# First layer of a graph propagation: blocks' places looked up half a round ahead, in PSUM banks of their own

## The reference

```python
def _propagate(all_emb, rows, cols, vals):
    acc = all_emb
    x = all_emb
    for _ in range(N_LAYERS):          # 3
        x = jax.ops.segment_sum(vals[:, None] * x[cols], rows, num_segments=N_NODES)
        acc = acc + x
    return acc / (N_LAYERS + 1)
...
rating = users_emb @ items_emb.T
rating = rating + bias_user[users] + bias_item.T
return jax.nn.sigmoid(rating)
```

## Time and profile before

| | us |
|---|---|
| median of 3 runs | 7561.97 |
| lowest and highest | 7558.92, 7563.39 |
| profiled execution | 7557.79 |
| its span | 7556.0 |

### The profile page before, as it was taken

The page is one execution under the profiler, slowest core; times in us unless marked ns, Lnnn a source line. Parts: engine busy times, 40 slices in busy tenths (PEclk is TensorE's granted clock), DMA queues, the critical chain, the costliest instruction groups (busy, mean ns, idle before and its releaser), DMA issues.

```text
span 7556.0 us, 213021 instructions
## 1 busy us (share of the span) xinstructions
PE 4726.8 (63%) x73184; PEld 4198.0 (56%) x73188; DVE 5009.9 (66%) x11593; ACT 4137.8 (55%) x10708; POOL 2330.0 (31%) x2100
## 2 busy tenths in 40 slices
PE   5201111057777777887566666788666666678879
PEld 4200110046666666887556666688655666668854
DVE  9999999964444445999544444599844444469970
ACT  0155445333333335999444444699744444479976
POOL 0144434034444443000454455200055555520000
PEclk9755555555556655555676666655577776665559
DMA  9300000034444444554344444455444444445536
GB/s 345 148 0 0 0 0 0 0 94 135 133 137 134 135 134 129 142 145 120 127 138 132 136 137 137 133 145 146 110 137 138 135 138 135 134 132 145 145 105 241
DMA packets 750538, 918.14 MB, mean 122 GB/s; under 512 B 71784, under 2 KB 607881, under 8 KB 750363
## 3 DMA queue, kind: packets, MB, share of 16 engines
q1 hardware_dynamic: 658540, 665.77, 31.9%
q0 software_dynamic: 91520, 250.84, 8.9%
q10 hardware_dynamic: 434, 1.05, 0.1%
HBM read 529.36 MB, written 388.09 MB: 121 GB/s over the span
## 4 chain that ended last, share of the span: by engine, by line
PE 34%; issue 23%; DVE 17%; DMA 11%; ACT 10%; another core or an unknown queue 2%; POOL 2%; DVEq 1%; ACTq 0%; SPq 0%; POOLq 0%
PE psum L1420 28%; DMA ring<-posts 11%; ACT ring L630 5%; ACT ring L628 3%; DVE store L987 3%; DVE store L985 2%; DVE total L817 2%; DVE store L995 2%; DVE store L996 2%; POOL ring L711 2%; PE psum L1415 2%; DVE ring L1174 1%; ACT ring L627 1%; PE psum L1471 1%
## 5 line engine op out<-in xcount | busy, mean ns | idle before, releaser
L1420 PE MATMUL psum<-ring 128*128 128x64 bf16 x45504 | 2524.4, 228 | 1187.7 <-issue 1077.5
L1420 PEld LDWEIGHTS psum<-ring 128*128 128x128 bf16 x45504 | 2256.0, 121 | 1437.2 <-issue 1411.9
L618 ACT ACTIVATE ring<-psum,ring 128x64 f32<-128x64 f32 x7584 | 1654.6, 340 | 2207.2 <-DVE ring L1197 889.8
L740 POOL DMA_INDIRECT posts<-ring x1896 | 1866.9, 985 | 1968.6 <-ACT ring L618 1531.6
L1170 DVE COPY ring<-store 128x384 bf16 x1896 | 522.2, 275 | 1472.6 <-PE psum L1420 714.5
L1174 DVE TENSOR_SCALAR ring<-ring,lane_f 128x512 bf16<-128x512 bf16 x3792 | 1177.7, 352 | 0.0
L1445 PE MATMUL psum<-ring 128*128 128x64 bf16 x15168 | 1002.6, 244 | 0.0
L1445 PEld LDWEIGHTS psum<-ring 128*128 128x128 bf16 x15168 | 965.1, 167 | 0.0
L630 ACT ACTIVATE ring<-ring 128x1024 bf16<-128x1024 uint8 x948 | 943.5, 1042 | 0.0
L1439 PE MATMUL psum<-ring 128*128 128x64 bf16 x7584 | 616.9, 249 | 238.4 <-ACT psum L634 224.8
L1439 PEld LDWEIGHTS psum<-ring 128*128 128x128 bf16 x7584 | 555.8, 158 | 302.5 <-issue 300.4
(11 more groups left out here) (239 smaller groups left out, 4207.9 us busy)
## 6 DMA issues: line engine op xcount, KB each, us to landing
ring<-posts SPq DMA_DIRECT2D x474, 516.0 KB, 3.9
ring<-lanes_d SPq DMA_DIRECT2D x474, 512.0 KB
out<-ring SPq DMA_DIRECT2D x200, 250.0 KB, 2.0
posts<-store SPq DMA_DIRECT2D x2, 20640.0 KB, 115.8
posts<-store SPq DMA_DIRECT2D x2, 20124.0 KB, 88.6
posts<-ring POOLq DMA_INDIRECT x1896
ring<-runs_d SPq DMA_DIRECT2D x158, 128.0 KB
user_rows<-total SPq DMA_DIRECT2D x1, 1568.0 KB, 5.9
```

The costliest lines, as they stand in the source:

```text
L618: last = nc.scalar.activation(of, psum[:, n, b * F:(b + 1) * F], ACT.Copy, scale=vring[:, h, c * BLOCK + b:c * BLOCK + b + 1])
L740: pool.indirect_dma_start(out=posts[:, :], out_offset=bass.IndirectOffsetOnAxis(ap=dring[:, h, c:c + 1], axis=0), in_=msg[:, n, :], in_off ...
L1420: last = pe.matmul(psum[:, n, b * F:(b + 1) * F], hot[c][:, k, b * P:(b + 1) * P], xt[c][:, (k * PARTS + x) * F:(k * PARTS + x + 1) * F], ...
```

## The change

In the first layer the look-up of a half's places moves ahead by half a round. VectorE makes the one-hot runs of the next half after the third one-hot block of this half; TensorE does the next half's look-up straight after this half's fourth sum, into bank 4 or 5 (by half), which no sum uses; VectorE reads the shifts after the half's own four one-hot blocks, without waiting for a sum, and writes the places to `dest_m`, from where they are copied to `dring` as in the other layers. So that banks 4 and 5 are free, the first layer's sums go to banks 0 to 3 in turn: TensorE waits for the message of four blocks back, not eight. The first look-up stands ahead of the loop, and the last round is written out behind it, since it has no next one. Layers 1 and 2 keep eight banks.

```diff
@@ ScalarE, messages
-                            last = nc.scalar.activation(of, psum[:, n, b * F:(b + 1) * F], ACT.Copy,
+                            last = nc.scalar.activation(of, psum[:, n if layer else c, b * F:(b + 1) * F], ACT.Copy,
@@ VectorE
+                def run_hots(h, landed, looked):
+
+                    dve.wait_ge(s_drow[h], landed)
+                    if looked is not None:
+                        dve.wait_ge(s_looked, looked)
+                    for k in range(2):
+                        last = nc.vector.tensor_scalar(rhot[h][:, k, :], runs_r[h], lane_f[:, k:k + 1], None, ALU.is_equal)
+                    last.then_inc(s_rhot, 1)
+
+                def place(i, h):
+
+                    dve.wait_ge(s_looked, i * 2 + (h + 1))
+                    nc.vector.tensor_reduce(found[:, h, :], psum[:, 4 + h, 0:4 * PARTS].rearrange("p (c x) -> p c x", x=PARTS),
+                                            AX.X, ALU.add).then_inc(s_found, 1)
+                    dve.wait_ge(s_found, i * 2 + (h + 3))
+                    nc.vector.tensor_tensor(dest_m[:, bass.ds(i * 8 + h * 4, 4)], found[:, h, :], order_m[:, bass.ds(i * 8 + h * 4, 4)],
+                                            ALU.add).then_inc(s_placing, 1)
+
-                            if layer == 0 and c == 0:
-                                dve.wait_ge(s_drow[h], i * 16 + 16)
-                                for k in range(2):
-                                    last = nc.vector.tensor_scalar(rhot[h][:, k, :], runs_r[h], lane_f[:, k:k + 1], None, ALU.is_equal)
-                                last.then_inc(s_rhot, 1)
+                            if layer == 0 and c == 2 and not (final and h == 1):
+                                run_hots(1 - h, i * 16 + 16 * (h + 1), None if first and h == 0 else i * 2 + h)
+                        if layer == 0:
+                            place(i, h)
                         dve.wait_ge(s_msg, i * 8 + (done + h * 4 + 4))
+                        if layer == 0:
+                            dve.wait_ge(s_placing, i * 2 + (h + 1))
                         if not first:
                             dve.wait_ge(s_scat[h], i * 64 + layer * BODIES * 64)
                         if layer == 0:
-                            dve.wait_ge(s_sent, i * 8 + (h * 4 + 5))
-                            nc.vector.tensor_reduce(found[:, h, :], psum[:, h * 4, 256:256 + 4 * PARTS].rearrange("p (c x) -> p c x", x=PARTS),
-                                                    AX.X, ALU.add).then_inc(s_found, 1)
-                            dve.wait_ge(s_found, i * 2 + (h + 3))
-                            nc.vector.tensor_tensor(dring[:, h, :], found[:, h, :], order_m[:, bass.ds(i * 8 + h * 4, 4)], ALU.add).then_inc(s_placing, 1)
-                            dve.wait_ge(s_placing, i * 2 + (h + 1))
-                            nc.vector.tensor_copy(dest_m[:, bass.ds(i * 8 + h * 4, 4)], dring[:, h, :])
-                        else:
-                            nc.vector.tensor_copy(dring[:, h, :], dest_m[:, bass.ds(i * 8 + h * 4, 4)])
+                            dve.sem_inc(s_dvepace, 1)
+                        nc.vector.tensor_copy(dring[:, h, :], dest_m[:, bass.ds(i * 8 + h * 4, 4)])
...
                 if layer == 0:
+                    run_hots(0, 16, None)
                     send(0, True)
-                with dve.Fori(0 if layer else 1, BODIES) as i:
-                    send(i, False)
+                    with dve.Fori(1, BODIES - 1) as i:
+                        send(i, False)
+                    send(BODIES - 1, False, True)
+                else:
+                    with dve.Fori(0, BODIES) as i:
+                        send(i, False)
@@ TensorE
-                with pe.Fori(0, BODIES) as i:
+                def look_up(i, h):
+
+                    _, at_d = nc.values_load_multi_w_load_instructions(
+                        super_d[0:1, bass.ds(i * 8 + h * 4, 4)], engines=(mybir.EngineType.PE,), min_val=0,
+                        max_val=(SUPERS - 1) * 2 * PARTS, skip_runtime_bounds_check_because="the chip clamps each above")
+                    pe.wait_ge(s_rhot, i * 2 + (h + 3))
+                    pe.wait_ge(s_found, i * 2 + (h + 1))
+                    for m in range(4):
+                        for k in range(2):
+                            last = pe.matmul(psum[:, 4 + h, m * PARTS:(m + 1) * PARTS], rhot[h][:, k, m * P:(m + 1) * P],
+                                             dflat[:, bass.ds(at_d[m] + k * PARTS, PARTS)], start=(k == 0), stop=(k == 1))
+                    last.then_inc(s_looked, 1)
+
+                def sums(i, final):
+
                     for n in range(8):
                         c = n % 4
-                        if layer == 0 and c == 0:
...
+                        bank = n if layer else c
                         pe.wait_ge(s_hots, i * 8 + (done + n + 9))
-                        pe.wait_ge(s_msg, i * 8 + (done + n + 1))
...
+                        pe.wait_ge(s_msg, i * 8 + (done + n + (1 if layer else 5)))
                         for b in range(BLOCK):
                             for k in range(2):
                                 for x in range(PARTS):
-                                    last = pe.matmul(psum[:, n, b * F:(b + 1) * F], hot[c][:, k, b * P:(b + 1) * P],
+                                    last = pe.matmul(psum[:, bank, b * F:(b + 1) * F], hot[c][:, k, b * P:(b + 1) * P],
                                                      xt[c][:, (k * PARTS + x) * F:(k * PARTS + x + 1) * F],
                                                      start=(k == 0 and x == 0), stop=(k == 1 and x == PARTS - 1))
                         last.then_inc(s_sent, 1)
+                        if layer == 0 and c == 3 and not (final and n == 7):
+                            look_up(i + n // 4, 1 - n // 4)
+
+                if layer:
+                    with pe.Fori(0, BODIES) as i:
+                        sums(i, False)
+                else:
+                    look_up(0, 0)
+                    with pe.Fori(0, BODIES - 1) as i:
+                        sums(i, False)
+                    sums(BODIES - 1, True)
```

15 lines of the change are left out of this document (3 added, 12 removed).

## The result

| | before, us | after, us |
|---|---|---|
| median of 4 runs | 7562.68 | 7447.61 |
| lowest and highest | 7558.92, 7575.33 | 7443.69, 7450.63 |
| span of the profiled execution | 7556.0 | 7446.2 |

After takes 0.9848 of the time of before, with a 95% interval of 0.9835 to 0.9860: 115 us or 1.5% faster.

A forecast was written before the change was run, and what follows sets the result against it. The prediction took the message loop to be bound by how fast TensorE gets instructions. Profiled execution 7557.8 us, 0 for the waits and +3 for one instruction gave 7561 us, no change; range 7508 to 7588.

The forecast's parts named there:

- The step that failed: Message loop: TensorE's instruction supply, 26.08 a microsecond, sets the round, so removing waits saves nothing.
- the equal rates: First layer's and layer 1's message loops both take 26.08 instructions a microsecond, read as a common limit.
- The prediction's last line: Closing caveat on the message loops: all of it would be wrong if the equal rates are chance.
- GpSimd was counted out by its busy share: First layer's stretch: GpSimd, busy 594 of 1300 us, was called far from full.
- the earlier ring: VectorE sets the ring 1.3 us to 3.8 us earlier; only fills ScalarE's and GpSimd's idle time, no gain.
- the waits ahead of the look-ups: TensorE's idle before look-ups, 0.67 us a round, goes; priced at 0, at most 53 us for 79 rounds.
- The first rival: First layer's loop: TensorE's look-up waits come off in full, 53 us, giving 7505 us; chance 0.24.
- The four banks: First layer's sums need message n-4, not n-8; between -0 and +0.85 us a half, taken as nothing.
- VectorE's new waits: VectorE waits for the runs' transfer after the third block and the look-up after the fourth; free unless nearly 3.8 us late.
- Layers 1 and 2 and the ends: Layers 1 and 2 not touched; at the ends of the first layer's loop, within 1 us.
- one more instruction a round: TensorE, first layer's loop: the second look-up's next-round indices cost perhaps one instruction a round, 3 us.
- the banks' rival: First layer: sums stand until their bank is read; 34 us, 7592, or 85 us, 7643; chance 0.09.

The follow-up runs named there:

- late-ring run: The changed kernel with one wait put back: VectorE waits for the half's first sum before placing; 7540.28 us, 0.9998 of before.
- bunched run: The changed kernel, but in the first layer GpSimd waits for a half's fourth message before issuing its four scatters; 7618.47 us, 1.0104 of before.
- spaced: The changed kernel; in all layers a half's first three scatters each also wait for the sum of the block behind; 7319.48 us, 0.971 of before.
- the one with semaphore steps: The changed kernel with six semaphore steps on GpSimd after each scatter; 7426.72 us, 1.0005 of before; on the fifth chip 6650.54 us, 1.0124.
- spaced kernel before: The kernel before, each half's first three scatters also waiting for the next block's sum; 7379.43 us, 0.994; on the fifth chip 6583.56 us, 1.0016.

## Why the prediction was wrong

**The step that failed** is the sentence "So I take the loop to be bound by how fast TensorE gets instructions, not by a wait". It rested on the equal rates, 26.08 a microsecond in two loops. Both loops issue eight scatters a round, and both are held up by them for about as long: 6.7 and 7.0 us of gaps a round in before. What the first layer's round has more, 2.16 us, is mainly its 16 look-ups, busy for 157.2/74 = 2.12 us; that these 2.16 us for 56 instructions come to 26 a microsecond too is chance. The prediction's last line named it. What the runs show in its place is GpSimd's scatters: with them gone, layer 1's round falls from 15.4 to 6.6 us and the rate goes to 61 a microsecond; with the change alone the first layer's goes to 28.4. GpSimd was counted out by its busy share (594 of 1300 us); but an engine at 46% can slow another one while it works. The profile of before could have refuted the step by itself: its instruction queues moved 44 packets in the whole execution and none in these stretches.

**From it followed the second error**: the earlier ring "fills ScalarE's and GpSimd's idle time only". The late ring made four messages come at once, and with them four scatters in a row; with the early ring the scatters follow the sums. The late-ring run shows that all of the gain hangs on VectorE's passing that wait earlier, the bunched run that scatters in a row are enough to undo it with the ring early. The term was priced at 0 and measured 7562.68 - 7447.61 = 115 us: 0.85 us a round of less standing and 0.57 of shorter time at work.

**Right:** the waits ahead of the look-ups went (0.67 to 0.18 us a round), and by themselves they give nothing: in the late-ring run they are down to 4.4 us of a stretch, the time is that of before (0.9998), and the idle has moved into the sums. What absorbs them is not a supply of instructions, though. The first rival, the waits in full, 53 us, is refuted by the same run, though its sign was that of the result. The four banks cost nothing (1.0002 alone); idle behind ScalarE is 2.0 us in after's stretch of 1200. VectorE's new waits are hidden, as expected: 73.2 us for the runs, 84 times, longest 2.0. They are hidden by what holds TensorE up, though; on the fifth chip, where that is missing, they grow to 212.7 us of 900 and TensorE waits behind VectorE. Layers 1 and 2 and the ends stayed.

**A term that was mis-sized:** one more instruction a round, 3 us. TensorE's sequencer hands out 458 a round in after as in before; the term is 0. A slip in the banks' rival: its 0.31 us of wait a half should be 49.6/148 = 0.34, which makes its 85 us 81; nothing hangs on it.

**What is not settled.** By which path GpSimd's requests hold TensorE up is not shown: 8-byte rows leave it, half the traffic leaves it, fewer requests relieve it, and one chip hardly has it. That the four messages of a half coming at once is what put the scatters in rows is read from the traces, and so is their share in rows. The share of scatters in rows goes with the time in most pairs (before and late ring against after, after against spaced), but not in all: the bunched kernel is slower than before at the same 96%, the one with semaphore steps slower than the change at a smaller share, layer 1 of before stands as long in gaps with 51% in rows as the first layer with 94%, and the spaced kernel before a little faster at an equal one. So a second thing in the scatters' timing acts beside it. Nor is it separated how much of the bunching acts by lengthening the idle pieces and how much by their timing, which the clock answers to; the spaced kernel gained by the clock alone, the bunched one lost by both. Why six semaphore steps cost 1.6% is open. The obvious next trial, one request for two blocks' rows, has not been run.

## What to carry to other kernels

An engine that is off the critical path, and half idle, can still slow the one on it: take its work away once (here, a semaphore step in place of the scatter) before calling the idle pieces of another a lack of instructions. Equal rates in two loops are evidence of a common limit only when the loops don't also share a neighbour. Where such a neighbour disturbs, tie its requests to the progress of the engine that matters, one by one: releasing four at once cost 2.6% of the change's time (1.0104 / 0.9848), and holding each back until the next sum was done won 1.4% on one chip; in the kernel before it won 0.6% on another and nothing on a third. And a wait that is hidden only because another engine is slow is not free: it came back as soon as that engine was not held up.

## What the hardware showed that I had not expected

- A scatter request of GpSimd (128 rows, about 1 us) costs TensorE 0.7 to 1.5 us a piece in layer 1. In the rows shown TensorE does one to three matmuls, then stands some 0.5 us, with a period of 0.72 us, until about 0.8 us after the last request; 632 of 634 gaps of the first layer's stretch lie at a scatter or less than 0.8 us behind one.
- In layer 1, TensorE's granted clock is 0.71 with eight scatters a round, 0.95 with four and 1.00 with none: the gaps cost their own length, and a second time in what runs between them at 1.2 in place of 2.4 GHz.
- The same kernel takes 7425 to 7563 us on most of the chips used and 6573 us on one, and on that one another engine sets the time. A change of 1.5% on the one kind says nothing yet on the other.
- In the loops' stretches the profile shows no packet on the instruction queues, so a TensorE that stands for "issue" in such a loop is not waiting for a fetch from memory.
